# First expert of a mixture-of-experts layer in two stages, the first of them on the slots of five of the seven token tiles

## The reference, cut to what matters

```python
x = _layernorm(x + _L0_attn_ref(x, W_Q, W_K, W_V, W_O))            # 16 heads of 128, causal
x = _layernorm(x + _L0_xattn_ref(x, ctx_2048, Wq, Wg, bg, Wkv, Wo))  # linear attention, gated
x = _layernorm(x + _L0_ffn_ref(x, router_weight, ...))

# _L0_ffn_ref: T = 896 tokens, E = 8 experts, two of them for each token
logits = h @ router_weight.T + router_bias
top_vals, top_idx = jax.lax.top_k(logits, 2)
top_w = jax.nn.softmax(top_vals, axis=-1)
scores = zeros_like(logits).at[arange(T)[:, None], top_idx].set(top_w)
gate_up = einsum('th,ehj->etj', h, gate_up_proj) + gate_up_proj_bias[:, None, :]
glu = gate * sigmoid(gate * 1.702)          # gate, up: every second column, clipped at 7
expert_out = einsum('eti,eih->eth', (up + 1.0) * glu, down_proj) + down_proj_bias[:, None, :]
out = einsum('te,eth->th', scores, expert_out)
```

## Time and profile before

| | |
|---|---|
| median of 3 runs | 877.49 us (874.13 to 878.26) |
| profiled execution | 877.32 us |
| its span, first to last instruction | 875.5 us |
| TensorE busy, weight loads busy | 827.1 us (94%), 726.2 us (83%) |
| VectorE, ScalarE, POOL busy | 471.7, 310.5, 102.7 us |
| mean granted TensorE clock | 0.974 |

### The profile page before, as it was taken

How to read it: one execution, slowest core, us unless ns; L and a number is a source line. 1 busy time by engine, 2 the same in 40 slices (tenths; PEclk the granted TensorE clock), 3 DMA queues, 4 the chain that set the end, 5 groups by cost and what they waited for, 6 DMA issues and landing times. The chain is left out here.

```text
span 875.5 us, 12501 instructions
## 1 busy us (share of the span) xinstructions
PE 827.1 (94%) x4878; PEld 726.2 (83%) x4878; DVE 471.7 (54%) x862; ACT 310.5 (35%) x700; POOL 102.7 (12%) x95
## 2 busy tenths in 40 slices
PE   7999999999999999999999999999988999999980
PEld 6999897989898898978899878888867888888860
DVE  4535454363635463575760344445577687777524
ACT  4443323243333432332443122211233465555430
POOL 0000000000000000000000000110131244443343
PEclk9999999999999999999999999999977999999995
DMA  9790724524020203003110001110376466656336
GB/s 329 261 292 6 243 90 152 175 67 134 6 97 6 97 8 121 3 4 132 50 36 1 25 12 36 60 60 1 111 301 196 143 186 192 198 172 172 76 38 186
DMA packets 35902, 97.91 MB, mean 112 GB/s; under 512 B 6648, under 2 KB 9080, under 8 KB 33152
## 3 DMA queue, kind: packets, MB, share of 16 engines
q1 hardware_dynamic: 32032, 88.62, 29.6%
q0 software_dynamic: 3808, 8.46, 5.0%
HBM read 64.03 MB, written 32.12 MB: 110 GB/s over the span
## 5 line engine op out<-in xcount | busy, mean ns | idle before, releaser
L306 PE MATMUL bank<-w_kv,cT 128*125 128x512 f32 x576 | 143.6, 400 | 0.9 <-DVE acc L1370 0.9
L306 PE MATMUL bank<-xT,w_qkv 128*128 128x512 f32 (+1 forms) x672 | 138.0, 365 | 2.1 <-ACT qT L1059 2.1
L306 PEld LDWEIGHTS bank<-xT,w_qkv 128*128 128x128 f32 x672 | 122.0, 188 | 17.4 <-issue 2.2
L306 PEld LDWEIGHTS bank<-w_kv,cT 128*125 128x125 f32 x576 | 104.1, 186 | 24.8 <-issue 1.3
L306 PE MATMUL bank<-x_g,w_gu 128*128 128x288 f32 x768 | 109.1, 300 | 3.6 <-DVE x_g L1336 2.9
L306 PEld LDWEIGHTS bank<-x_g,w_gu 128*128 128x128 f32 x768 | 104.9, 191 | 5.5 <-issue 3.2
L470 POOL TENSOR_TENSOR ln_rs<-ln_ve,half 128x1 f32<-128x1 f32 (+2 forms) x16 | 12.7, 792 | 630.4 <-DVE ln_ve L1465 630.3
L306 PE MATMUL bank<-w_o,zT 128*128 128x512 f32 x336 | 79.8, 395 | 0.5 <-DVE acc L1671 0.5
L306 PE MATMUL bank<-w_qkv,xT 128*128 128x256 f32 x588 | 77.3, 287 | 0.0
L306 PEld LDWEIGHTS bank<-w_o,zT 128*128 128x128 f32 x336 | 61.7, 188 | 15.0 <-DVE acc L1370 1.8
L306 PEld LDWEIGHTS bank<-w_qkv,xT 128*128 128x128 f32 x588 | 72.2, 191 | 0.0
(11 more groups left out here) (150 smaller groups left out, 1156.0 us busy)
## 6 DMA issues: line engine op xcount, KB each, us to landing
x_rows<-blank SPq DMA_DIRECT2D x9, 2084.0 KB, 16.5
raw_gu<-in_w_gu_dram SPq DMA_DIRECT2D x8, 2048.0 KB
raw_w<-in_w_qkv_dram SPq DMA_DIRECT2D x22, 512.0 KB, 7.0
raw_dn<-in_w_down_dram SPq DMA_DIRECT2D x8, 1024.0 KB
raw_c<-in_ctx_t_dram SPq DMA_DIRECT2D x8, 750.0 KB, 4.3
raw_o<-in_w_o_dram SPq DMA_DIRECT2D x8, 512.0 KB, 3.7
xg<-x_rows SPq DMA_DIRECT2D x8, 512.0 KB, 6.5
raw_kv<-in_w_kv_dram SPq DMA_DIRECT2D x2, 1024.0 KB, 7.0
```

The source lines that it names most:

```text
L306: last = nc.tensor.matmul(mm_out, lhs(a, k), rhs(b, k), start=(k == 0 and i == 0), stop=(k == n - 1 and i == 2))
```

## The change

Expert 0 is computed in two stages, A and B (`STAGES`). Its slots are laid out anew: tokens of the first five tiles (`EARLY`) take slots 0 to 223 (`CAP_A`), those of the last two tiles slots 224 to 319 (`CAP_B` = 96). For this the running count of expert 0 restarts before tile 5 at a fixed value, slots of expert 0 that would go past 223 are moved on by 256 (`over`), and all other experts move by `SHIFT` = 32 rows. The counts of both parts go into the test for further rounds (`used`, `first_n`). Five pieces of code change their order with it:

- SP waits for the ten scatters of the first five tiles and loads their slots right behind the gate/up weights of expert 0, ahead of the gate/up weights of expert 1 and both down weights; the last piece of expert 0 comes when all scatters are done.
- TensorE gathers the first two pieces after `router(6)` and starts stage A: 96 products of 224 columns. `rank(6)`, `count`, `turn_scores(1)` and five `down_bias` stand between and behind its quarters. Then `gather(0, 2)` and stage B: 96 products of 96 columns, with the gathers of expert 1 and the last two `down_bias` between the quarters. The down products of expert 0 are one of 128 slots and two of 96.
- VectorE: `choose(4)` ahead of `sums_out(7)`, `assign(4)` ahead of `gated(7)`; two weight splits ahead of `x2_norm(5)` and `x2_norm(6)`; `choose(6)`, `assign(6)` behind the split of the gathered rows; `levels` and the bias adds among the operations of the stages.
- POOL makes two of the four low parts of the gate/up weights of expert 0 (`first_low`) and the low part of the down bias.
- The splits of the weights of expert 1 move into stage A and the first quarter of B (`SPLITS`), and the buffers of the hidden values of expert 0 are its own (`gl0` to `hh0`, `x_b`, `h_b`).

```diff
 PIECES = ((0, 128), (128, 128), (256, 32))
+EARLY, CAP_A, CAP_B = 5, 224, 96
+PIECES_0 = ((0, 128), (128, CAP_A - 128), (CAP_A, CAP_B))
+SHIFT = CAP_A + CAP_B - CAP
...
                 yield what, n, 6 + i % 2
-            last = [("rk", 4), ("st", 0), ("t1", 5), ("rt", 5), ("t1", 6), ("rk", 5), ("rt", 6), ("db", 0), ("rk", 6),
-                    ("cnt", 0), ("db", 1), ("db", 2), ("st", 1), ("db", 3), ("db", 4), ("db", 5), ("db", 6)]
-            for i, (what, n) in enumerate(last):
-                yield what, n, (6, 4, 5, 7)[i % 4]
+            last = [("rk", 4, 6), ("st", 0, 4), ("t1", 5, 6), ("rt", 5, 4), ("t1", 6, 6), ("rk", 5, 4), ("rt", 6, 6),
+                    ("rk", 6, 4), ("cnt", 0, 6), ("st", 1, 4), ("db", 0, 7), ("db", 1, 5), ("db", 2, 6), ("db", 3, 7),
+                    ("db", 4, 6), ("db", 5, 7), ("db", 6, 6)]
...
-        SPLITS = {0: ((3,), (), (), (), ()), 1: ((), (), (), (0,), (1, 2, 3))}
-
-        def splits_at(e, q):
-            if e + 1 == NE:
+        SPLITS = {0: ((), (0,), (1,), (2,), ()), 1: ((3,), (), (), (), ()), 2: ((), (), (), (0,), (1, 2, 3))}
+
+        def splits_at(s, q):
+            if s == NE:
                 return ()
-            return SPLITS[e][q] if e in SPLITS else (q,) if q < KC else ()
+            return SPLITS[s][q] if s in SPLITS else (q,) if q < KC else ()
...
-            return 4 + (3 * e + k) % 2 if e or k < 2 else 0
+            return 4 + (3 * e + k) % 2 if e else (1, 3, 4)[k]
...
+            sp.wait_ge(row_out_a, 16 * 2 * EARLY)
+            sp.dma_start(xg[0][:, 0, :], x_rows_of(0, P)[:, 0:D]).then_inc(in_xa, 16)
+            sp.dma_start(xg[0][0:CAP_A - P, 1, :], x_rows_of(P, CAP_A - P)[:, 0:D]).then_inc(in_xa, 16)
+            sp.wait_ge(*ready("wo", NT - 1))
+            sp.dma_start(raw_gu[1], t["w_gu"][1]).then_inc(in_gu[1], 16)
...
-            sp.wait_ge(*ready("wo", NT - 1))
-            sp.dma_start(raw_gu[1], t["w_gu"][1]).then_inc(in_gu[1], 16)
...
-            sp.wait_ge(row_out, 16 * 2 * NT)
-            for e in range(3):
-                rows_in(xg[e], e * ROWS, in_xg[e])
-            by_expert = x_rows.rearrange("(e r) l -> r e l", e=NE)
-            for k, (p0, rows) in enumerate(PIECES):
-                sp.dma_start(meta[0:rows, k], by_expert[p0:p0 + rows, :, D:L]).then_inc(in_meta, 16)
+            sp.wait_ge(row_out, 16 * 2 * (NT - EARLY))
+            sp.dma_start(xg[0][0:CAP_B, 2, :], x_rows_of(CAP_A, CAP_B)[:, 0:D]).then_inc(in_xg[0], 16)
+            for e in range(1, 3):
+                rows_in(xg[e], SHIFT + e * ROWS, in_xg[e])
+            by_expert = x_rows[SHIFT:SHIFT + NE * ROWS, :].rearrange("(e r) l -> r e l", e=NE)
+            for k in range(3):
+                p0, rows = PIECES_0[k]
+                sp.dma_start(meta[0:rows, k, 0], x_rows_of(p0, rows)[:, D:L]).then_inc(in_meta, 16)
+                p0, rows = PIECES[k]
+                sp.dma_start(meta[0:rows, k, 1:NE], by_expert[p0:p0 + rows, 1:NE, D:L]).then_inc(in_meta, 16)
...
-                    sp.wait_ge(m["gu_mm"], KC * (e + 1))
+                    sp.wait_ge(m["gu_mm"], KC * (e + 2))
                     sp.dma_start(raw_gu[e % 2], t["w_gu"][e + 2]).then_inc(in_gu[e % 2], 16)
...
+            def first_low(k):
+                pool.wait_ge(m["gu_hi"], k + 1)
+                nc.gpsimd.tensor_tensor(w_gu[0][:, 1, k], raw_gu[0][:, k], bits(w_gu[0][:, 0, k]), ALU.subtract)\
+                    .then_inc(m["gu_lo"], 1)
+
             for n in range(1, 5):
                 inverse_std(1, n, n + 1, n + 3)
                 scatter(n - 1)
+            scatter(4)
             inverse_std(1, 5, 6, 8)
-            scatter(4)
+            first_low(2)
             inverse_std(1, 6, 7, 9)
+            first_low(3)
+            pool.wait_ge(m["dnb_hi"], 1)
+            nc.gpsimd.tensor_tensor(dn_b[1][0:NE, :], raw_dnb[0:NE, :], bits(dn_b[0][0:NE, :]), ALU.subtract)\
+                .then_inc(m["dnb_lo"], 1)
             scatter(5)
             scatter(6)
...
+            rank(4)
             cross_out(5, 1, 3)
             turn_atn(7)
             cross_out(5, 3, KC)
-            rank(4)
             turn_scores(0)
             cross_out(6)
             turn_x2(5)
             router(5)
             turn_x2(6)
-            rank(5)
-            router(6)
-            down_bias(0)
-            rank(6)
-            count()
-            down_bias(1)
-            down_bias(2)
...
+                    pe.wait_ge(in_xa, 32)
+                elif i == 2:
+                    pe.wait_ge(in_xg[0], 16)
...
+                if (e, k) == (0, 2):
+                    down_piece(w_dn[0], h_b, 0, rows, y_bank(e, k))
+                else:
+                    down_piece(w_dn[e % 2], hT[e % 2], p0, rows, y_bank(e, k))
+
+            rank(5)
+            router(6)
+            gather(0, 0)
+            gather(0, 1)
+            for k in range(4):
...
+            for s, (part, e) in enumerate(STAGES):
                 pe.wait_ge(m["gu_lo"], KC * e + KC)
-                pe.wait_ge(m["xg_lo"], 3 * e + 3)
+                pe.wait_ge(m["xg_lo"], 2 if part == "A" else 3 * e + 3)
                 for q in range(KC):
-                    gate_up_part(e, w_gu[e % 2], x_g[e % 2], q)
-                    if e == 0 and q + 1 < KC:
+                    gate_up_part(s, w_gu[e % 2], rows_of_stage(s), q)
+                    if part == "A" and q == 0:
+                        rank(6)
+                        count()
+                    if part == "A" and q == 1:
+                        turn_scores(1)
+                        down_bias(0)
+                    if part == "A" and q == 2:
+                        down_bias(1)
+                        down_bias(2)
+                    if part == "B" and q + 1 < KC:
                         gather(1, q)
+                    if part == "B" and q in (1, 2):
+                        down_bias(4 + q)
                     if q and e and e + 1 < NE:
                         gather(e + 1, q - 1)
-                if e == 0:
+                if part == "A":
+                    down_bias(3)
+                    down_bias(4)
+                    gather(0, 2)
+                if e == 1:
                     for k in range(6, 8):
                         pe.wait_ge(free[k], LAST[k])
-                else:
+                if e:
                     for k in range(3):
                         down(e - 1, k)
             for k in range(3):
...
@@ -1568,11 +1642,20 @@
                 dve.wait_ge(*ready("rk", n))
                 nc.vector.tensor_tensor(pos[:, s, :], bank("rk", n)[:, 0:NE], offs[:, :], ALU.add)\
                     .then_inc(done("rk", n)[0], 1)
+                if 1 <= n < EARLY:
+                    dve.wait_ge(*done("rk", n))
+                    nc.vector.tensor_scalar(over[:, :], pos[:, s, 0:1], float(CAP_A), float(2 * P), ALU.is_ge, ALU.mult)\
+                        .then_inc(m["over_ok"], 1)
                 dve.wait_ge(m["tw_ok"], n + 1)
                 dve.wait_ge(m["dif_ok"], n + 1)
                 nc.vector.scalar_tensor_tensor(sc2[:, s, :], dif[:, s, :], tw[:, s:s + 1], chosen[:, s, :],
                                                ALU.mult, ALU.add).then_inc(m["sc_ok"], 1)
                 dve.wait_ge(*done("rk", n))
+                if 1 <= n < EARLY:
+                    dve.wait_ge(m["over_ok"], 2 * n - 1)
+                    nc.vector.tensor_tensor(pos[:, s, 0:1], pos[:, s, 0:1], over[:, :], ALU.add)\
+                        .then_inc(m["over_ok"], 1)
+                    dve.wait_ge(m["over_ok"], 2 * n)
                 nc.vector.tensor_tensor(prod[:, s], hot[:, s], pos[:, s, :].unsqueeze(1).to_broadcast([P, 2, NE]),
                                         ALU.mult).then_inc(m["prod_ok"], 1)
...
                 if b == 5:
                     assign(3)
+            choose(4)
             sums_out(7)
-            choose(4)
             attended(7)
+            assign(4)
             gated(7)
             cross_add(5)
             a_low(7)
             cross_stats(5)
```

More of the change, by code:

```diff
@@ L521, in add_rows @@
                         .then_inc(add_done, 16)
+            for q in range(KC):
+                gated(0, q)
             for e in range(NE + 1):
@@ L923, in _, with gathered @@
             turn_x2(6)
-            rank(5)
-            router(6)
-            down_bias(0)
-            rank(6)
-            count()
-            down_bias(1)
-            down_bias(2)
-            turn_scores(1)
-            for n in range(3, NT):
-                down_bias(n)
-            def gathered(c, src, k, bk):
-                p0, rows = PIECES[k]
+            def gathered(src, k, rows, bk):
                 for i in range(KC):
@@ L1270, in scaled @@
+            def scaled(c, k, rows, bk, slot, weight):
                 act.wait_ge(m["dn_mm"], 3 * c + (k + 1))
@@ L1309, in _ @@
                     y_evac(e - 1, 1)
-                if more:
+                if more and part != "A":
                     dn_high(e, e % 2)
@@ L1775, in _ @@
```

(9 more changed lines are left out.)

342 lines of the change are left out of this document (186 added, 156 removed).

## The result

The changed kernel takes **903.1 us** (median of 4 runs, 900.86 to 905.89) against 877.41 us of the kernel before: a ratio of 1.0289, 95% interval 1.0258 to 1.0321, slower by 2.9%. Forecast were 882.1 us and a range up to 888.0 us. The direction was right and the size wrong by 21 us. The profiled execution took 904.13 us, its span is 902.3 us: 26.8 us more than before, of which the forecast had 4.8.

The account below looks back on a forecast made before the run. TensorE carries the span, with a 24.8 us hole without expert products. Stage terms sum to 35.9 us from 652.4 us, so the second expert starts at 688.3, 4.8 us later: 877.3 + 4.8 = 882.1 us; range 873.5 to 888.0 us.

Parts of the forecast that it names:

- from there to stage A: From cross_out(6) through routing, weight splits and transposes to stage A: 14.0 us, first product at 652.4 us.
- 224 columns at full clock: Stage A's 96 products of 224 columns: 107 ns each, 10.3 us.
- half clock in stage A: Start of stage A: clock back after 5.0 us, 27 products at 187 instead of 107 ns, 2.1 us.
- three waits: down_bias(4) for its bank 2.4 us, gather(0, 2) ahead of stage B 1.3, expert 1's last piece 1.3: 5.0 us.
- stage B's 96 products: Stage B's products of 96 columns: pace set by loading 128 columns of weights, 110 ns each, 10.6 us.
- rival of the lost clock: Clock falls again between the stages: 26 products at 190 instead of 110 ns, 884.8 us; put at 886.5 us, chance 0.22.
- highest case: Bias products between the quarters also keep the clock low throughout the first stage: 888.5 us.
- short rows of the price: Stage B's pace from short trace groups: 112 columns 114 ns, transposes 88 ns, router's 8 columns 122 ns; 110 ns taken.
- lower bound: Stage B at 88 ns, clock back after 3.4 us, waits halved: 5.4 us less, 876.7 us.
- held clock: Rival: router(6) ends by 646 us, first stage starts at 648.0 us without half clock: 872.8 us, chance 0.11.
- Hidden weight loads: Rival: weight loads hide in stage B, 53 ns a product, 5.1 instead of 10.6 us: 878.7 us, chance 0.22.
- extra round: Rival: expert 0's slots overflow; 182 and 78 tokens fit 224 and 96 slots, so none added, no chance set aside.

Follow-up runs that it names:

- b_at_once: Changed kernel with late rows gathered within stage A's last quarter and two bias products moved into stage B, so B follows A without gap: 899.4 us, 1.0245.
- splits_dve: Changed kernel with all weight and bias splits of expert 0 on VectorE, none on POOL: 898.3 us, ratio 1.0246.
- mid96: Kernel before, with expert 3's 96 gate/up products moving 96 columns instead of 288: 883.5 us, ratio 1.0059.
- all_three_128: As all_three, but stage B's products move 128 columns instead of 192: 890.2 us, ratio 1.0165.
- b_wide224: Changed kernel with stage B's products moving 224 columns (the first stage's rows) instead of 96: 889.9 us, ratio 1.0142.
- all_three: Changed kernel with stage B straight after A, no splits on POOL, and stage B's products moving 192 columns: 881.5 us, ratio 1.0051.
- all_three_warm: As all_three, plus 15 unread products of 128 x 512 in TensorE's waits between cross_out(6) and stage A: 884.0 us, ratio 1.0058.
- staged_warm_256: As all_three_warm, but stage B's products move 256 columns instead of 192: 878.3 us, ratio 1.0017.
- deep_bias: Kernel before, with its 21 bias products over 128 rows, 120 of them zeros, instead of 8: 878.6 us, ratio 1.0000.

## Why the prediction was right or wrong

By its own steps, in the profiled execution; up to the end of expert 1's first 48 products the changed kernel is 27.7 us behind (717.57 against 689.91 us), 22.9 us more than the 4.8 forecast, and the rows below give 21.9 of them. Behind that point 0.9 us is won back, which leaves the 26.8 us at the end.

| step | forecast | measured | adds |
|---|---|---|---|
| work before `cross_out(6)` that isn't the change | 0 | 1.9 us | 1.9 |
| `cross_out(6)` later | 0.4 us | 0.56 us | 0.2 |
| from there to stage A | 14.0 us | 18.9 us | 4.9 |
| 224 columns at full clock | 107 ns | 120 ns, 24 in 2.87 us | 1.2 |
| half clock in stage A | 2.1 us | 1.6 us, 24 in 4.51 us | -0.5 |
| three waits | 5.0 us | 1.60 + 1.21 + 1.25 us | -0.9 |
| stage B's 96 products | 110 ns, 10.6 us | 213 ns, 20.9 us with the steps between banks | 10.3 |
| other work in stage B | at full clock | two bias products 0.7 us longer each, transposes 0.9 us | 2.3 |
| expert 1's first 48 products | as before | 9.09 us | 2.5 |

- **The failed step** is the one for stage B, "I take 110 ns: 10.6 us". The pace at full clock was about right (116 ns in b_at_once, single starts 112 ns apart). What failed is that it was taken at full clock: the sum let the clock come back once, in stage A, and stay. With the two rows below it this is 15.1 of the 22.9 us; the 224-column run gave 13.2 us back.
- **The rival of the lost clock** named the right place, the 5 us of bias products and transposes between the stages, and the direction. Its price was wrong, "26 products at 190 instead of 110 ns": it let 96-column products bring the clock back as 288-column ones had. They neither bring it back nor hold it; the gap it argued from isn't even needed. Its highest case, 888.5 us, lay 15 us short, and has a slip: the 5.5 + 2.9 - 2 us that "come on" to 884.8 give 891.2 us.
- **The earlier trace rows had shown it**, and I read them too mildly: TensorE all but always busy from 645 to 660 us, at half clock, among 8-row bias products. I took the small work for cut-up work. That the products themselves may be too thin was to be asked of stage B as well. The Trainium skill, "TensorE: Matmul & The Clock Gate", part 1, ties the fall to idle time and the return to sustained work; here a busy TensorE lost the clock (0.52 in 735 to 737 us, no gap), so the measurement decides.
- **Start of stage A.** POOL's splits were sized rightly (2.33 us, forecast 2.2). But I let them hold only `choose(5)`, for 0.9 us. They held both normalisations (2.0 us each), and VectorE's splits held POOL's inverse deviations. Without them the stretch took 14.6 us (splits_dve), near the 14.0 forecast. The Trainium skill, "SBUF — State Buffer", section "SBUF: two separate sides", excludes GpSimd not only against two SBUF inputs, which I used, but also against VectorE's two-port modes; a normalisation from SBUF to SBUF, 2.57 us beside POOL and 0.55 us alone, agrees with that, though no run here shows its mode.
- **The short rows of the price** were read too coarsely, and 110 ns is partly luck. The prediction divided the length of short groups by their count, gaps and edges with it. The single starts in the same trace lie 109 ns apart for the transposes (it read 88), 112 for the router (122) and 98 for most of the 112-column products, whose weights have 112 columns too (114). So the 88 ns under its lower bound and its held clock was no pace of this trace.
- **Hidden weight loads and held clock** are out: in mid96, 96-column products start 112 ns apart at full clock (but for the first pair, 43 ns), far from the rival's 53 and the quoted 43 ns, and A's first product came at 659 us at half clock. That rows landing near 646 us weren't what stage A waits for held: they are used at 656.22 us.
- **The extra round** didn't occur. After expert 1 little changed, as said: from its first 48 products to the end the 27.7 us became 26.8.

## What to carry to other kernels

Before a stage is cut into pieces, ask of every piece's matmuls how wide and how deep they are. Here 96 columns cost what 224 cost at full clock (single starts 112 ns apart), and they took the clock down for themselves and for what followed. Padding was free: unread columns beside the thin products, rows of zeros under the shallow ones. Read the clock again in each stretch after the change, not only where the old kernel lost it. An operation that is given to an idle POOL is not free while VectorE works from SBUF to SBUF on the critical path.

## What of the hardware was unexpected

- The granted clock under a TensorE that was busy throughout: it fell to half among 96-column products alone (mid96), and where bias products stood between the quarters, with 96 and with 128 columns by 128 rows (b_at_once, all_three_128). It came back from half among products of 224 and of 288 columns (b_wide224, before). With 192 columns it held in one kernel's profiled run (all_three) and was lost in most runs of another (all_three_warm, 877 or 884 us); with 256 it fell for 3.4 us (staged_warm_256). In these three, bias products stood between the quarters as well; what their part was stays open.
- Bias products of 8 rows by 512 columns left it at half from 651 to 660 us; the same products with 120 rows of zeros began at 648 us and had it back at 653 us. Zeros are enough for that.
- At full clock single starts lie 112 ns apart for 96, 192 and 224 columns and 120 ns for 256; at half clock 213 ns for 96, 128, 192, 224 and 256 columns alike, and 240 ns for 288.
- A wait of 2.5 us without any product (657.5 to 660 us in deep_bias) left the clock at 1.00. The wait for expert 1's last piece did not always: 1.77 us in both before and mid96, but in mid96's profiled execution the clock fell at 684 us, as in deep_bias's after 1.86 us, and the first 48 products took 8.15 instead of 6.63 us. A single profiled execution can differ by 1.5 us through this alone.
